# A second list made one layer earlier, a short block wholly on its list, and one update moved: a change to a four-layer graph network kernel

## What is computed

```python
# layer 2: attention, softmax over the neighbours; the diagonal and other entries differ by 1e9 * (1 - adj)
e = (s_i[:, None, :] + s_j[None, :, :]) * scale + ((1.0 - adj) * -1e9)[:, :, None]
out = einsum('ijh,jhd->ihd', softmax(e, axis=1), xp)
# layer 3: a message per edge, summed with the edge's weight, then an update
s, d = x @ msg_w[:, :D].T, x @ msg_w[:, D:].T
messages = gelu(s[:, None, :] + d[None, :, :] + msg_b)
aggregated = einsum('ijd,ij->id', messages, adj)
h = gelu(concatenate([x, aggregated]) @ upd_w.T + upd_b) + x
x = layernorm(x + (layernorm(h) * ln_w + ln_b))
```

## Time and profile before

| | |
|---|---|
| three runs | 754.19, 753.02, 754.19 us; median 754.19 |
| span of the profiled execution | 758.7 us |
| DVE busy | 505.2 us (67%) |
| PE busy | 461.8 us (61%) |
| POOL busy | 376.7 us (50%) |
| ACT busy | 302.4 us (40%) |
| DMA | 120.07 MB, mean 158 GB/s |

### The profile page before, as it was taken

The page is one execution under the profiler, slowest core; times in us unless marked ns, Lnnn a source line. Parts: engine busy times, 40 slices in busy tenths (PEclk is TensorE's granted clock), DMA queues, the critical chain, the costliest instruction groups (busy, mean ns, idle before and its releaser), DMA issues.

```text
span 758.7 us, 6873 instructions
## 1 busy us (share of the span) xinstructions
PE 461.8 (61%) x1987; PEld 273.2 (36%) x1987; DVE 505.2 (67%) x1592; ACT 302.4 (40%) x362; POOL 376.7 (50%) x499
## 2 busy tenths in 40 slices
PE   5222016999959999999994586545524642484111
PEld 4121013444425565454463464333313431342110
DVE  2509806998944547983344845999797779777744
ACT  2665255457742331898553230132323222322213
POOL 7204610766650303763003746577777777776640
PEclk9555555899989999999998569677656665655555
DMA  8999992999940202799002221111122122212200
GB/s 325 353 425 419 397 381 39 368 415 390 392 186 0 74 0 76 283 404 421 13 14 78 73 71 49 31 52 49 52 52 56 45 55 54 55 46 56 52 15 14
DMA packets 33212, 120.07 MB, mean 158 GB/s; under 512 B 8704, under 2 KB 19892, under 8 KB 24148
## 3 DMA queue, kind: packets, MB, share of 16 engines
q1 hardware_dynamic: 20258, 80.99, 27.1%
q0 software_dynamic: 10176, 38.57, 16.3%
q10 hardware_dynamic: 2734, 0.01, 0.2%
HBM read 114.00 MB, written 5.55 MB: 158 GB/s over the span
## 4 chain that ended last, share of the span: by engine, by line
PE 34%; POOL 22%; DMA 20%; issue 11%; DVE 6%; ACT 3%; another core or an unknown queue 1%; SPq 1%; ACTq 0%; POOLq 0%
PE ps L121 33%; DMA ring<-in_adjT_dram 18%; POOL G L919 17%; POOL Go L919 5%; DMA G<-near,IX 2%; ACT binT L1001 1%; PE ps L1257 1%; PE ps L1263 1%; DVE M L1703 1%; SPq L822 0%; DVE X L1696 0%; DVE E L1797 0%; ACTq L1004 0%; DVE st L1687 0%
## 5 line engine op out<-in xcount | busy, mean ns | idle before, releaser
L919 POOL DMA_INDIRECT G<-near,IX x154 | 159.6, 1036 | 58.3 <-issue 49.7
L121 PE MATMUL ps<-ring,hwu 128*128 128x512 f32 (+3 forms) x264 | 114.8, 588 | 1.0 <-ACT hwu L1014 1.0
L121 PE MATMUL ps<-ring,xT_s 128*128 128x512 f32 (+2 forms) x264 | 106.9, 547 | 2.0 <-DMA ring<-in_adjT_dram 2.0
L121 PE MATMUL ps<-ident,agg 128*128 128x128 f32 (+1 forms) x44 | 15.9, 461 | 135.6 <-DVE agg L1827 105.2
L1503 DVE FIND_INDEX8 I<-V,rows 128x8 uint32<-128x340 f32 (+2 forms) x176 | 88.1, 504 | 0.0
L1513 DVE MAX8 V<-rows 128x8 f32<-128x340 f32 (+2 forms) x176 | 85.5, 496 | 0.8
L121 PE MATMUL ps<-E,M 128*128 128x321 f32 (+2 forms) x192 | 65.6, 502 | 22.8 <-DVE IO L1719 15.3
L121 PEld LDWEIGHTS ps<-ring,hwu 128*128 128x128 f32 (+1 forms) x264 | 51.4, 204 | 64.4 <-issue 63.3
L1001 ACT ACTIVATE binT<-ring 128x2708 bf16<-128x2708 f32 (+1 forms) x22 | 53.9, 2457 | 44.1 <-DMA ring<-in_adjT_dram 44.1
L942 POOL DMA_DIRECT2D rows<-in_adj_dram x18 | 10.9, 603 | 120.6 <-DVE I L1503 120.6
L1021 ACT ACTIVATE binT<-ring 128x2708 bf16<-128x2708 f32 (+1 forms) x22 | 54.0, 2456 | 37.5 <-PE ps L121 28.4
(11 more groups left out here) (255 smaller groups left out, 859.1 us busy)
## 6 DMA issues: line engine op xcount, KB each, us to landing
ring<-in_adjT_dram SPq DMA_DIRECT2D x48, 1354.0 KB, 16.9
rows<-in_adj_dram POOLq DMA_DIRECT2D x17, 1354.0 KB, 10.2
rows<-in_adj_dram SPq DMA_DIRECT2D x4, 1354.0 KB, 23.4
G<-near,IX POOLq DMA_INDIRECT x154
xT_s<-in_xT_dram SPq DMA_DIRECT2D x1, 1354.0 KB, 6.6
near<-hwu SPq DMA_DIRECT2D x1, 1344.0 KB
out_dram<-yo SPq DMA_DIRECT2D x21, 64.0 KB
near2f<-hwu SPq DMA_DIRECT2D x5, 256.0 KB
```

The source lines that it names most:

```text
L121: return pe.matmul(dst, lhsT, rhs, start=start, stop=stop, skip_group_check=True)
L919: pool.indirect_dma_start(out=dst, out_offset=None, in_=table, in_offset=bass.IndirectOffsetOnAxis(ap=index, axis=0), engine_sem=o_g).then ...
```

## The change

It has four parts.

- The masks of pair 1 are made right after those of pair 0 in layer 2; PE multiplies its list in its turn for group 2 of GROUPS2, 193 columns wide; DVE takes the list before `normal2` of group 4. At the start of layer 3 `own_shares_listed(1)` multiplies the own shares of pair 1 into the list's bank, and DVE copies them to ownL under a new semaphore, v_own, for which PE waits before it makes list 2.
- POOL waits for v_opre only from pair 2 on, and for the pair before the one it waited for.
- Block 21 has all its entries on the list of its pair (`tensor_copy` in the place of `match_replace`). Its seven gathers, its adds and its multiply and reduce over eight places are gone; what is left is the diagonal's place.
- In the last pair block 21 comes first (`pair3`, and `turn3` for the semaphore counts). `update(9)` stands between the two blocks of the last pair, as every update before it.

```diff
+        def pair3(g):
+
+            return (2 * g, 2 * g + 1) if g < NG3 - 1 else (2 * g + 1, 2 * g)
+
+        def turn3(n):
+            return 2 * (n // 2) + pair3(n // 2).index(n)
+
+        def first_slot(n):
+            return 0 if n < NB - 1 else TOP
...
@@ gpsimd
             for g in range(NG3):
                 pool.wait_ge(v_list, g + 1)
-                if g:
-                    pool.wait_ge(v_opre, g)
+                if g >= 2:
+                    pool.wait_ge(v_opre, g - 1)
                 all_begun(NB + (2 * TOP + CAP) * g)
                 for k in range(CAP):
                     gather(Go[:, g % 2, k, :], near3[:, :], IO[:, g, k:k + 1], s_go[g % 2])
-                for n in (2 * g, 2 * g + 1):
+                for n in range(2 * g, min(2 * g + 2, NB - 1)):
@@ scalar
             for g in range(NG3):
+                n, later = pair3(g)
                 messages_listed(g)
-                messages(2 * g)
-                if 0 < g < NG3 - 1:
+                messages(n)
+                if g:
                     deviations3(g - 1)
-                messages(2 * g + 1)
+                messages(later)
                 aggregated(g)
-                if g == NG3 - 1:
-                    deviations3(g - 1, 0, 1)
                 features(g)
-            deviations3(NG3 - 2, 1, 2)
             deviations3(NG3 - 1)
@@ tensor
+                if g == 2:
+                    pe.wait_ge(v_own, 1)
-                w = LISTED if g else EDGE
+                w = LISTED if g > 1 else EDGE
...
                 if g == 0:
                     pe.wait_ge(c_pr, CH)
                     lists(0)
+                if g == 2:
+                    lists(1)
                 pe.wait_ge(v_x3, g + 1)
...
-            def own_shares_listed():
+            def own_shares_listed(g):
 
                 for k in range(CAP):
-                    for n in range(2):
-                        last = mm(pe, bank(3, k * D, D), M[:, n, k * P:(k + 1) * P], E2[:, n, EDGE:LISTED], n == 0, n == 1)
+                    to = list_bank[:, k, EDGE:LISTED] if g else bank(3, k * D, D)
+                    for i in range(2):
+                        n = 2 * g + i
+                        last = mm(pe, to, M[:, n, k * P:(k + 1) * P], E2[:, n, EDGE:LISTED], i == 0, i == 1)
                 last.then_inc(p_opre, 1)
...
             own_shares(0)
             own_shares(1)
-            own_shares_listed()
-            lists(1)
+            own_shares_listed(0)
+            own_shares_listed(1)
@@ vector
-                dve.match_replace(edges[0:r, n, SEGS * 8:2 * SEGS * 8], T8[0:r, n, :], V, 0.0)
+                if n < NB - 1:
+                    dve.match_replace(edges[0:r, n, SEGS * 8:2 * SEGS * 8], T8[0:r, n, :], V, 0.0)
+                else:
+                    dve.tensor_copy(edges[0:r, n, SEGS * 8:2 * SEGS * 8], V)
...
             dve.wait_ge(c_pr, CH)
             rows_to_list(0)
+            rows_to_list(1)
             take_list(0)
             for g, (first, count) in enumerate(GROUPS2):
+                if g == 4:
+                    take_list(1)
                 normal2(g, first, count)
...
@@ before_gelu
-                dve.tensor_tensor(G3[0:r, q, TOP, :], pd3[0:r, n, 0:D], own, ALU.add)
+                alone = dve.tensor_tensor(G3[0:r, q, TOP, :], pd3[0:r, n, 0:D], own, ALU.add)
+                if first_slot(n) == TOP:
+                    alone.then_inc(v_pre, 1)
+                    return
@@ aggregate
+                if first_slot(n) == TOP:
+                    dve.wait_ge(p_agg, turn3(n) - 1)
+                    dve.tensor_scalar(agg[0:r, n % 2, :], at[:, TOP, :], T8[0:r, n, TOP:TOP + 1], None, ALU.mult).then_inc(v_agg, 1)
+                    return
...
             dve.wait_ge(c_d, len(GROUPS2))
-            rows_to_list(1)
             rows_to_list(2)
             list_to_rows(0)
-            take_list(1)
+            dve.wait_ge(p_opre, 2)
+            dve.tensor_copy(ownL[:, 1, :, :], list_bank[:, :, EDGE:LISTED]).then_inc(v_own, 1)
             for g in range(NG3):
+                n, later = pair3(g)
                 listed_before_gelu(g)
-                before_gelu(2 * g)
+                before_gelu(n)
...
-                aggregate(2 * g)
-                if 0 < g < NG3 - 1:
+                aggregate(n)
+                if g:
                     update(g - 1)
-                before_gelu(2 * g + 1)
+                before_gelu(later)
...
-                aggregate(2 * g + 1)
+                aggregate(later)
...
-            update(NG3 - 2)
             dve.wait_ge(v_out, NG3 - 1)
             update(NG3 - 1)
```

More of the change, by code:

```diff
@@ L298, in build @@
         v_rank, v_M, v_list, v_A, v_win, v_x3 = sem("v_rank"), sem("v_M"), sem("v_list"), sem("v_A"), sem("v_win"), sem("v_x3")
+        v_own = sem("v_own")
         v_h, v_out, v_s, v_pre, v_agg, v_opre = sem("v_h"), sem("v_out"), sem("v_s"), sem("v_pre"), sem("v_agg"), sem("v_opre")
@@ L1143, in messages @@
             def messages(n):
-                act.wait_ge(v_pre, n + 1)
-                at = G3[0:rn(n), n % QUEUE3, :, :]
+                act.wait_ge(v_pre, turn3(n) + 1)
+                at = G3[0:rn(n), n % QUEUE3, first_slot(n):, :]
                 act.activation(at, at, ACT.Gelu).then_inc(c_msg, 1)
@@ L1425, in aggregate @@
                 r = rn(n)
-                pe.wait_ge(v_agg, n + 1)
-                mm(pe, bank(SUMS, n % 2 * P, r), agg[0:r, n % 2, :], ident[0:r, 0:r], False, n % 2 == 1).then_inc(p_agg, 1)
+                pe.wait_ge(v_agg, turn3(n) + 1)
+                mm(pe, bank(SUMS, n % 2 * P, r), agg[0:r, n % 2, :], ident[0:r, 0:r], False, turn3(n) % 2 == 1).then_inc(p_agg, 1)
             def new_features(g):
@@ L1446, in _ @@
                 aggregate_listed(g)
-                aggregate(2 * g)
-                aggregate(2 * g + 1)
+                for n in pair3(g):
+                    aggregate(n)
                 if g + 2 < NG3:
@@ L1711, in take_list @@
                 few.done(dve.tensor_copy(listed[:, :, :], list_bank[:, :, 0:EDGE]))
-                if g:
+                if g > 1:
                     dve.tensor_copy(ownL[:, g % 2, :, :], list_bank[:, :, EDGE:LISTED])
@@ L1822, in aggregate @@
                 r, at = rn(n), G3[0:rn(n), n % QUEUE3, :, :]
-                dve.wait_ge(c_msg, n + 1)
+                dve.wait_ge(c_msg, turn3(n) + 1)
+                if first_slot(n) == TOP:
+                    dve.wait_ge(p_agg, turn3(n) - 1)
+                    dve.tensor_scalar(agg[0:r, n % 2, :], at[:, TOP, :], T8[0:r, n, TOP:TOP + 1], None, ALU.mult).then_inc(v_agg, 1)
+                    return
                 few.done(dve.tensor_tensor(at, at, T8[0:r, n, :].unsqueeze(2).broadcast_to([r, TOP + 1, D]), ALU.mult))
                 if n >= 2:
-                    dve.wait_ge(p_agg, n - 1)
+                    dve.wait_ge(p_agg, turn3(n) - 1)
                 dve.tensor_reduce(agg[0:r, n % 2, :], at.rearrange("p k d -> p d k"), AX.X, ALU.add).then_inc(v_agg, 1)
```

## The result

The changed kernel takes 747.31 us (median of 8 runs, 742.39 to 748.31), the kernel before 753.59 beside it (8 runs, 749.59 to 755.95). The ratio is 0.9907, with a 95% interval of 0.988 to 0.9933: 7.0 us faster. Forecast were 747.6 us and a range of 741 to 751.

A forecast was written before the change was run, and what follows sets the result against it. The prediction took POOL's queue of row gathers in layer 3 as the bound. Hand-over +6.65, hole -0.7, block 21 with update(9) -8.8 and tail -3.7 sum to -6.55: 754.19 becomes 747.6 us, range 741 to 751.

The forecast's parts named there:

- Parts 2 and 3, the hand-over: Layer 2 into layer 3: making pair 1's list early delays the first listed gather by 6.65 us, from 4.2 to 7.4.
- PE's list: Layer 2, ahead of group 2's transposes: 16 matmuls take 4.77 us and delay ACT's deviations of group 3 by 3.95.
- rival C: Layer 2 hand-over: costs 4.2 us instead of 6.65 since PE's clock rises; 745.2 us, chance 0.13.
- take_list's own +2.7: Layer 2, DVE before group 4: taking the list lasts 3.28 us, less 0.59 idle, so 2.7 later.
- Part 4, the hole: Start of layer 3: POOL no longer waits for pair 1's messages, 0.7 us saved, by the profile 7.0.
- Parts 5 and 6: End of layer 3: block 21's seven gathers go and update(9) moves before block 20's add; the add starts 8.8 us earlier.
- the 1.0 us of extra gap at 715.70: POOL near the end of layer 3: this extra gap goes too without the late signal at 716.23.
- Part 1, the masks: Layer 2: pair 1's masks, 3.0 us in all, fall into DVE's idle 4.95 before take_list(0) and cost nothing.
- I take it as likeliest that both belong to the profiled execution alone: Layer 3: DVE's two waits on "remote", 8.32 us before pair 1's COPY and 2.92 near the end, are absent from the runs.
- the first of the two sums: POOL's hole at the start of layer 3, reckoned for runs without the late signal: 0.7 us, against 7.0 by the profile.
- rival B: Layer 3: the late signals are in the runs too, so -10.95 us, 743.2; chance 0.22.
- Rival D: Layer 2, group 2's transposes: PE's next signal comes 8.3 us late, hand-over 15.0, time 756.0; chance 0.03.

The follow-up runs named there:

- e8: Early list alone against the kernel before: pair 1's list made in layer 2, block 21 and update(9) unchanged; third chip, 764.45 us, ratio 1.0039.
- e5: Block 21 alone against the kernel before: on the list, no gathers; pair 1's list late, update(9) at the end; second chip, 744.37 us, ratio 0.9883.
- e6: update(9) alone against the kernel before: moved between the last pair's blocks, block 21 keeps its gathers; second chip, 750.06 us, ratio 0.9972.
- e1: Early list alone against the kernel before: pair 1's list made in layer 2, block 21 and update(9) unchanged; first chip, 784.83 us, ratio 1.0234.
- run 128: Not a follow-up run or kernel: the words come from "that run 128 columns wide", the dense run of 32 matmuls at layer 3's start; no time of its own.
- e11: The whole change, but PE multiplies pair 1's list right after pair 0's; DVE still takes it before group 4; fourth chip, 763.74 us, ratio 0.9977.
- e2: Tail alone against the kernel before: block 21 on the list, update(9) moved, pair 1's list made in layer 3; first chip, 749.9 us, ratio 0.9874.
- e3: The whole change, but PE multiplies pair 1's list right after pair 0's and DVE takes it after the loop; first chip, 767.79 us, ratio 1.0071.
- e7: The changed kernel without an edit, run again on the third chip; 751.08 us, ratio 0.9875 against the kernel before.

## Why the prediction was right, and where it was not

- **The time.** 747.6 was forecast and 747.31 measured, and the parts at the end agree: block 21 alone 8.8 us (9.2 by the two landings), update(9) alone 2.1 (2.2; interval 0.4 to 3.8), the tail from add to last update 3.64 in the profile (3.7). The early list alone was never run on a chip with signals on time; its price there is read from the profile.
- **Parts 2 and 3, the hand-over:** +6.65 forecast, +5.65 measured (45.75 less 40.10). The term that was mis-sized is PE's list: 3.67 us, not 4.77, because the granted clock rose to 1.00 while it ran. That is the mechanism of rival C, at about two fifths of its size (C's 4.2 would have been 2.45 less than the forecast, and it was 1.0); in `e8` the hand-over, 43.28, is 2.94 over that of before on the same chip (40.34). Group 3's deviations came 2.56 later (437.59 for 435.03) instead of 3.95, which by the prediction's own 4.8 less 0.9 should have read 3.9, and the first listed gather at 453.72 instead of 455.0. The place and the mechanism held, the 2.98 us idle of DVE behind ACT included. take_list's own +2.7 held in kind (3.18 less what DVE idled there).
- **Part 4, the hole:** 0.7 without a late signal; the profile of `e5` shows 0.8.
- **Parts 5 and 6:** -8.8 forecast for the add, -9.53 measured in the profile. update(9) was done just before the landing, so the add waited for the landing after all, by 0.18. One credit in the sum was wrong: the 1.0 us of extra gap at 715.70 was laid to the late signal, but POOL's gap of 1.32 at this place is in the profiles without late signals too (the change at 716.21, `e5` at 709.78, `e6` at 705.74). Without it the landing would have set part 6, at -9.2.
- **Part 1, the masks:** they took DVE's idle time (its wait before take_list(0) fell to 2.50), and a gather beside them took 1.34 at most; nothing of it reached the end. The prediction's 1.24 us gather is a weak sign for the shared port: the next one, at 411.88, ran beside the same operations and took 0.99.
- **What failed** is the step "I take it as likeliest that both belong to the profiled execution alone". Late signals recur, and with them the times of all runs beside them, on three of the four chips of the experiments: before runs at 760 where its profile has them, and at 753 on the second chip, where the profiles of `e5` and `e6` have none. The two profiled executions of before that have them, 759.93 and 758.97, stand at the medians beside them, 760.21 and 759.5; if they belonged to these two executions alone, the two would be some 6 us above. So the 6.2 us between the profiled execution of before and the median of its three runs fit a second chip; which chip that execution ran on isn't known, and this last step is argued. The prediction put the 2.92 us wait at 716.23 beside it; by the trace's semaphore events that one was for DVE's own multiply, ended at 713.31 and signalled at 716.21. For PE's list, where the prediction saw no second clue, the same trace has the signal itself, at 474.10, right before DVE's start. That the number survived is in part luck: the runs of the result were made where signals are on time, for which the first of the two sums holds. The parts as measured add to -8.3 (5.65 - 0.8 - 9.5 - 3.6), inside the interval of the -7.0 that the runs show (-5.0 to -9.0); errors of 1 us in single terms are below what these runs can tell. On a chip with late signals the forecast of rival B, -10.95, is nearer to what was measured (-9.5 on the third chip).
- The Trainium skill (Perfetto Trace Analysis, Summary: the profiler window per engine type), that the end shown for a matmul is an estimate and the passing on of a semaphore hidden, was cited in the prediction and set aside. The runs agree in that the recorded end doesn't tell when the signal comes: the same 6.27 us of matmuls have their consumer start 0.04 us after it in `e5` and 6.3 us after it in the earlier trace rows.
- Rival D, late signals inside layer 2, wasn't seen; in layer 3 it was, and in kernel `e1` it cost far more than D's 8.3.

**What stays open.** What makes signals late on some chips. The longest are PE's, and their first long one in each such profile comes behind the dense run of small matmuls at the start of layer 3. With the early list, which makes all 32 matmuls of that run 128 columns wide, the waits there are 7.6 to 21.9 us, with the late list 8.0 to 9.1. No kernel changed the pace of that run, so this is a coincidence seen, not a cause shown. Nor are PE's the only ones: DVE's own signal came 2.9 us late in the earlier trace rows, and in `e11` ACT waited 4.03 for one of DVE's.

The traces hold a sign that comes earlier than that run and parts the two kinds of profile without exception. Before 400 us each of the fourteen has 2563 to 2604 semaphore events. From there on the three without late signals (the change, `e5`, `e6`) have 5000 to 5111 and the eleven with them 2276 to 2661; the first missing one is at 419 to 430 us, in layer 2, while the instructions themselves are on record. So the profiles with late signals are those whose recording lost events. Whether recording delays the engines on those chips, or one thing does both, no run separates; since no run is known to be free of recording, that rival stands.

Nor was the whole change measured on the chip where `e1` lost 24.6 us (17.8 by the ratio), and `e2` and `e3` were not measured where signals are on time; by the sum of the parts, an early list out of the way or none should be some 4 to 5 us better than the change there, an estimate.

**The best version.** On the first chip the tail alone (`e2`, 749.9) beat before by 1.26%, with the narrowest spread there, 748.44 to 753.07. The whole change did as well on the third chip (0.9875). Where signals are on time, block 21 alone (`e5`, 0.9883) did no worse than the whole change (0.9907), without an early list; the intervals overlap and the chips are not known to be the same. No kernel here is shown to beat the change on one chip.

## What to carry to other kernels

Work that is put into an in-order chain of engines to close a hole later is paid at the hand-over of that chain; here 5.65 us in the profile for a hole of 0.8 on a chip with signals on time. What paid was to take transfers off the queue that sets the time (8.8 us for seven gathers of 20 rows), and to move an update into a wait before the last landing. Before a wait in a profile is called the profiler's, the same kernel's own time should be held against runs on the same chip: a span that is longer than the runs allow may come from another chip. And before it is called the chip's, it is worth counting the semaphore events of both traces.

## What was not expected of the hardware

- A PE signal can reach its waiter long after the recorded end of the matmul that gives it. Before the COPY at the start of layer 3, DVE starts 5.8 us (`e7`) to 19.9 us (`e11`, 472.60 to 492.50) after that end in the profiles from three chips, and 0.04 us after it in `e5` and the changed kernel's. All profiles with late signals are also short of semaphore events, 2276 to 2661 of some 5000.
- With them the spread mostly grows: runs of one kernel on one chip from 748.36 to 755.7 without (before, second chip), and from 762.72 to 781.68 (`e3`) or 755.69 to 786.03 (before, fourth chip) with them; but `e2`, with a wait of 9.1 us, keeps to 748.44 to 753.07.
- The same 16 matmuls of 128 x 193 took 5.48 us at a granted clock of 0.50, 3.67 at 0.75 and 2.78 at 1.00.
